# Row fetches that address x by bytes, with two rooms each, in a gather-bound graph layer

## The reference, cut to what matters

```
all_msgs = einsum('nh,thd->ntd', h, message_W) + message_b     # 8 edge types
msg      = all_msgs[src, edge_type]
messages = segment_sum(msg, dst, num_segments=12500)
gi = messages @ gru_w_ih.T + gru_b_ih ;  gh = h @ gru_w_hh.T + gru_b_hh
r = sigmoid(i_r + h_r); z = sigmoid(i_z + h_z); n = tanh(i_n + r * h_n)
out = layernorm(h + (1 - z) * n + z * h)
```

## Time and profile before

| | |
|---|---|
| median of three runs | 2633.79 us |
| span of the profiled execution, first to last instruction | 1973.7 us |
| the profiled execution's own time | not given by the page |
| median less span | 660.1 us |
| busy: POOL (GpSimd), PE (TensorE), DVE (VectorE), ACT (ScalarE) | 75%, 69%, 63%, 30% |
| share of the 16 DMA engines | about 25% |

### The profile page before, as it was taken

How to read it: one execution, slowest core, us unless ns; L and a number is a source line. 1 busy time by engine, 2 the same in 40 slices (tenths; PEclk the granted TensorE clock), 3 DMA queues, 4 the chain that set the end, 5 groups by cost and what they waited for, 6 DMA issues and landing times.

```text
span 1973.7 us, 39661 instructions
## 1 busy us (share of the span) xinstructions
PE 1356.7 (69%) x6561; PEld 1050.8 (53%) x6657; DVE 1248.0 (63%) x4650; ACT 594.6 (30%) x1489; POOL 1474.7 (75%) x1565
## 2 busy tenths in 40 slices
PE   1766676767676767676767676766667776767676
PEld 1755555555555555555555555555555554555554
DVE  7788366656565656565656565666566665656565
ACT  2423523232323232323232323232232323232322
POOL 7777777777777777777777777777777777777774
PEclk9878778888888888888888888888788888888888
DMA  5222222222222222222222222222222222222221
GB/s 128 59 63 64 60 61 65 64 66 64 66 65 64 66 62 67 62 67 62 67 63 66 62 67 63 65 65 65 65 65 65 65 65 65 65 65 64 65 63 42
DMA packets 103994, 128.78 MB, mean 65 GB/s; under 512 B 35152, under 2 KB 78495, under 8 KB 103806
## 3 DMA queue, kind: packets, MB, share of 16 engines
q0 software_dynamic: 49696, 101.88, 20.6%
q1 hardware_dynamic: 50328, 23.94, 4.4%
q10 hardware_dynamic: 3782, 0.93, 0.2%
HBM read 120.16 MB, written 6.40 MB: 64 GB/s over the span
## 4 chain that ended last, share of the span: by engine, by line
POOL 65%; issue 22%; DVE 8%; PE 3%; ACT 1%; DMA 1%; DVEq 0%; SPq 0%; ACTq 0%; POOLq 0%
POOL rows L697 32%; POOL rows_other L697 32%; DVE work L1354 1%; DVE codes L1351 1%; PE agg L1691 1%; DVE onehot L1187 1%; PE msg L1718 1%; DMA work<-in_src_dram 0%; PE msg L1836 0%; DVE root_a L1261 0%; DVE messages_T L1203 0%; ACT sums_room L763 0%; PE turn L1773 0%; ACT agg L763 0%; DVEq L1194 0%
## 5 line engine op out<-in xcount | busy, mean ns | idle before, releaser
L697 POOL DMA_INDIRECT rows<-in_x_dram,src_T x843 | 800.2, 949 | 258.8 <-issue 256.5
L697 POOL DMA_INDIRECT rows_other<-in_x_dram,src_T x675 | 638.1, 945 | 205.9 <-issue 205.9
L1691 PE MATMUL agg<-onehot,rows 128*128 128x128 f32 x1714 | 288.3, 331 | 250.1 <-DMA rows<-in_x_dram,src_T 248.5
L1718 PE MATMUL msg<-sums_room,w_type 128*128 128x320 f32 (+1 forms) x1552 | 439.9, 439 | 11.4 <-issue 7.1
L1691 PEld LDWEIGHTS agg<-onehot,rows 128*128 128x128 f32 x1714 | 259.8, 236 | 270.2 <-issue 269.1
L1691 PE MATMUL agg<-onehot,rows_other 128*128 128x128 f32 x1350 | 224.6, 326 | 230.5 <-DMA rows_other<-in_x_dram,src_T 229.0
L1718 PEld LDWEIGHTS msg<-sums_room,w_type 128*128 128x128 f32 x1552 | 302.6, 203 | 121.3 <-issue 27.2
L1236 DVE SCALAR_TENSOR_TENSOR sums_room<-turn,x_turned 128x128 f32<-128x128 f32 x696 | 145.8, 282 | 309.5 <-PE turn L1737 309.5
L1691 PEld LDWEIGHTS agg<-onehot,rows_other 128*128 128x128 f32 x1350 | 200.9, 231 | 248.2 <-issue 248.1
L763 ACT ACTIVATE sums_room<-agg 128x512 f32<-128x512 f32 x293 | 173.2, 591 | 364.4 <-PE agg L1691 264.3
L1187 DVE TENSOR_TENSOR onehot<-code_T,codes 128x640 f32<-128x640 f32 (+1 forms) x294 | 245.2, 863 | 18.2 <-PE agg L1691 18.2
(11 more groups left out here) (221 smaller groups left out, 1333.3 us busy)
## 6 DMA issues: line engine op xcount, KB each, us to landing
rows<-in_x_dram ACTq DMA_DIRECT2D x1792, 0.5 KB
w_hh_rows<-in_x_dram SPq DMA_DIRECT2D x1664, 0.5 KB
rows<-in_x_dram,src_T POOLq DMA_INDIRECT x843, 2.6
rows_other<-in_x_dram,src_T POOLq DMA_INDIRECT x675
x_next<-in_x_dram SPq DMA_DIRECT2D x97, 64.0 KB
out_dram<-out_tile SPq DMA_DIRECT2D x97, 64.0 KB
x_tile<-in_x_dram SPq DMA_DIRECT2D x96, 64.0 KB
work<-in_dst_dram SPq DMA_DIRECT2D x1, 609.4 KB
```

What stands on the lines that cost most here:

```text
L697: nc.gpsimd.indirect_dma_start(out=to, out_offset=None, in_=x[:, :], in_offset=bass.IndirectOffsetOnAxis(ap=index, axis=0),).then_inc(done ...
L1691: last = nc.tensor.matmul(agg[c][:, ds(offs[c][k] * TYPES, CODES)], tile_rows, onehot[c][:, k, :], start=False, stop=True, skip_group_chec ...
L1718: nc.tensor.matmul(msg[:, 0:cols], w_type[:, t, :], sums[:, t, 0:cols], start=t == 0, stop=False, skip_group_check=True)
```

## The change

1. The copies that make the tables of row numbers multiply them by 512 (`scale=float(ROW_BYTES)`), and there are two tables, `fetch_src` for ScalarE and `sync_src` for SyncE, since the two engines now fetch tiles of different places. SyncE waits for both (`fetch_src_ready, 2`).
2. A fetch takes 512 bytes of x, seen as a row of bytes, from the register's value on, and writes 512 bytes to the room.
3. Each engine has two rooms, used in turn.
4. SyncE's tile is place 7 (in group 1) instead of 15. ScalarE's stays at place 15. The rounds stay the same: 17, 23, ..., 95 and 20, 26, ..., 92. In a group TensorE takes the fetched tile last.
5. The rows are shared out over the blocks in another way: of the twelve blocks from the second one of a target round to the first one of the next, ScalarE weighs 5 (first) and 3 (second), SyncE 1 and 2, rounded to fours. That gives ScalarE 12 or 16 rows in a first block and 8 in a second (12 twice), SyncE 8 in a first and 12 or 16 in a second (8 ahead of round 20). Work on a first tile starts in the second block of round 12.
6. The waits that guard a room are for the tile before last: `tiles_done[2]` at the target of m-2, plus one.

```
+    ROW_BYTES = 4 * P
+    FETCH_STEPS, SYNC_STEPS = (6,), (6,)
+    FETCH_FIRST, SYNC_FIRST = EARLY + 6, EARLY + 9
+    FETCH_SHARE, SYNC_SHARE = (5, 3), (1, 2)
+    FETCH_PLACES, SYNC_PLACES = (15, 11, 7), (7, 15, 11)
...
+    def share_rows(rounds, share):
+        shares, before = {}, EARLY + 1
+        for m, target in enumerate(rounds):
+            places = [(r, half) for r in range(before, target + 1) for half in (0, 1)][1:-1]
+            weight, done, a = sum(share[half] for _, half in places), 0, 0
+            for place in places:
+                done += share[place[1]]
+                b = P * done // weight // 4 * 4
+                shares[place] = (m, a, b)
+                a = b
...
+        x_bytes = x.rearrange("n d -> (n d)").bitcast(U8)
-        sync_room = w_hh_rows[:, 0, :]
+        sync_rooms = [w_hh_rows[:, 0, :], w_hh_rows[:, 1, :]]
+        fetch_rooms = [rows[:, SPARE_SLOT, :], w_hh_rows[:, 2, :]]
...
-                        copy(fetch_src[0:ROWS, :], src_words[:, FETCH_SLOT * P:(FETCH_SLOT + 1) * P]).then_inc(fetch_src_ready, 1)
+                        for to, slot in ((fetch_src, FETCH_SLOT), (sync_src, SYNC_SLOT)):
+                            nc.scalar.activation(to[0:ROWS, :], src_words[:, slot * P:(slot + 1) * P], ACT.Copy,
+                                                 scale=float(ROW_BYTES)).then_inc(fetch_src_ready, 1)
...
             def fetch_rows(r, behind):
-                m, step = divmod(r - EARLY - 1, FETCH_EVERY)
...
+                m, begin, end = FETCH_SHARES[r, behind]
+                if begin == 0:
                     act.wait_ge(fetch_index_in[m % 2], (m // 2 + 1) * 16)
-                    act.dma_start(rows[p:p + 1, SPARE_SLOT, :], x[ds(number, 1), :]).then_inc(fetched[m % 2], 16)
+                    if m > 1:
+                        act.wait_ge(tiles_done[2], FETCH_ROUNDS[m - 2] + 1)
+                for a in range(begin, end, LOADED):
...
+                        act.dma_start(fetch_rooms[m % 2][p:p + 1, :].bitcast(U8),
+                                      x_bytes[ds(first, ROW_BYTES)].rearrange("(o n) -> o n", o=1)).then_inc(fetched[m % 2], 16)
...
             def gather_packed(r):
-                    for k in range(start, start + n - (c == 2 and (fetches(r) or sync_fetches(r)))):
+                    for k in range(start, start + n):
+                        if k - start in fetched_tiles(r, c):
+                            continue
...
             def sum_tiles(r, c, offs):
+                apart = fetched_tiles(r, c)
+                for k in [k for k in range(n) if k not in apart] + apart:
```

More of the change, by code:

```diff
@@ L9 @@
 I32 = mybir.dt.int32
+U8 = mybir.dt.uint8
 ALU = mybir.AluOpType
@@ L430, in fetches, with fetched_tiles @@
             return isinstance(r, int) and r in FETCH_ROUNDS
+        def fetched_tiles(r, c):
+            places = (fetch_place(r),) * fetches(r) + (sync_place(r),) * sync_fetches(r)
+            return [place - START[c] for place in places if START[c] <= place < START[c] + GROUPS[c]]
         def other(r):
@@ L581, in sync_rows @@
                     if m > 0:
-                        sp.wait_ge(tiles_done[2], r)
-                        if m + 1 < len(SYNC_ROUNDS):
+                        sp.wait_ge(tiles_done[2], SYNC_ROUNDS[m - 1])
+                        if m > 1:
+                            sp.wait_ge(tiles_done[2], SYNC_ROUNDS[m - 2] + 1)
+                        if m + 1 < len(SYNC_ROUNDS) and m > 0:
                             load_sync_index(m + 1)
-                _, numbers = nc.values_load_multi_w_load_instructions(
-                    sync_index[0:1, m % 2, a:a + n], engines=[sp.engine], min_val=0, max_val=NODES - 1,
-                    skip_runtime_bounds_check_because="row numbers, as the gathers take them")
@@ L588, in sync_rows @@
-                for p, number in enumerate(numbers, a):
-                    sp.dma_start(sync_room[p:p + 1, :], x[ds(number, 1), :]).then_inc(sync_fetched[m % 2], 16)
+                for a in range(begin, end, LOADED):
+                    _, numbers = nc.values_load_multi_w_load_instructions(
+                        sync_index[0:1, m % 2, a:min(a + LOADED, end)], engines=[sp.engine], min_val=0,
+                        max_val=(NODES - 1) * ROW_BYTES,
+                        skip_runtime_bounds_check_because="first bytes of rows, whose numbers the gathers take")
+                    for p, first in enumerate(numbers, a):
+                        sp.dma_start(sync_rooms[m % 2][p:p + 1, :].bitcast(U8),
+                                     x_bytes[ds(first, ROW_BYTES)].rearrange("(o n) -> o n", o=1)).then_inc(sync_fetched[m % 2], 16)
@@ L622, in _ @@
                     round_(r)
-                sp.wait_ge(fetch_src_ready, 1)
+                sp.wait_ge(fetch_src_ready, 2)
                 sp.wait_ge(bias_in, PARTS * 16)
@@ L1666, in landed @@
                 alike = range(EARLY + other(r), r + 1, 2)
-                left_out = sum(fetches(q) or sync_fetches(q) for q in alike) if c == 2 else 0
+                left_out = sum(len(fetched_tiles(q, c)) for q in alike)
                 return (0 if other(r) else (EARLY - 2) * EARLY_GROUPS[c]) + len(alike) * GROUPS[c] - left_out
```

81 lines of the change are left out of this document (48 added, 33 removed).

## The result

| | before | after |
|---|---|---|
| median, us | 2632.6 | 2452.85 |
| runs, lowest to highest | 4, 2624.72 to 2634.89 | 4, 2441.25 to 2468.42 |
| ratio after / before, 95% interval | | 0.9327 [0.9273, 0.9381] |

The change makes the kernel 6.7% faster, 180 us. I had forecast 2634.0 us and no change, with a range of 2622 to 2641 us.

The account below looks back on a forecast made before the run. GpSimd's gathers, 1.252 us each, were taken as the bound, hiding the fetches' saving. Span 1973.7 + 0 + 0.2 (one more copy at the start) = 1973.9 us, plus 660.1 us carried over, gave 2634.0 us; range 2622 to 2641 us.

Parts of the forecast that it names:

- the sum: Whole kernel: span 1973.7 + 0 + 0.2 = 1973.9 us, plus 660.1 us outside the span carried over, gives 2634.0 us.
- the cover: Fetch rounds: ScalarE's and SyncE's fetch issuing lies hidden behind GpSimd's gathers, so its saving is worth 0 us.
- cases of 0.06 each: Three rivals at 0.06 each: dearer byte fetches (2926 us), fetch issuing that counts (2516 us), 660 us growing with instructions (2577 us).
- GpSimd waits for nobody: From 241.84 to 1929.11 us GpSimd bounds: 1348 gathers by 1.252 us, with only one wait, of 1.9 us.
- The byte addresses: ScalarE's and SyncE's fetches: the multiplication goes, 70 ns saved per fetch, 0.378 to 0.308 us; worth 0 us, being hidden.
- The price of an instruction: At each fetch: FUSED_REGOPS of 37 ns plus its gap of 33 ns, 70 ns in all.
- Number of gathers, place, packets: 1553 tiles gathered before and after; SyncE's place 7 costs 0; two packets per fetch on q10 if the byte view is unsplit.
- Rooms and shares: Fetch blocks: two rooms with older guards, and other row shares with one more register load, all hidden, 0 us.
- C: Rival, faster: ScalarE's and SyncE's issuing counts in the timed execution; 118 us go, 2516 us; chance 0.06.
- D: Rival, faster: the 660 us grow with instructions; 3456 fewer is 8.7%, 57 us, giving 2577 us; chance 0.06.
- B: Rival, slower: the byte view makes each DMA_DIRECT2D longer, ScalarE's first block enters the loop; far end 2926 us; chance 0.06.
- A: The forecast itself: no change, 2634 us, as GpSimd's gathers bound the kernel; chance of same 0.77.

Follow-up runs that it names:

- six versions: Changed kernel (0.9327), it without fetches (0.9191), with ScalarE's alone (0.9213), with place 15 (0.9328), without fetches plus SyncE no-operations (0.9316); kernel before with byte addresses alone (0.9337).
- the probes: Separate programs doing none of the reference's work: no-operations alone, or beside GpSimd's gathers, loads, single-row transfers or small computing; starts counted, no ratio to the kernel before.
- the straight probe: Separate program of no-operations alone, written out, 1200 per engine in each of five stretches; 3340 starts in 40 us, none held.
- the probe of loops: The same no-operations in five stretches, each engine's 1200 as a loop of 12 times 100; none held, longest 18 ns from 160 to 200 us.

## Why the prediction was wrong, point by point

**The step that failed** is in the sum: "no row says what that is. I carry it over unchanged", of the 660.1 us between the span and the median. There is no such part. The profile of the same kernel among its timed runs has a span 1.7 us short of its time, and rounds of 26.1 us where I had read 19.5. With that the cover fell, too, behind which the sum put the fetches' saving at 0 us: the gathers of GpSimd, which I took for the bound, wait for the others in the timed runs. A missing quarter of the time was a reason to doubt the whole reading; I gave it to cases of 0.06 each.

**What bounds the kernel.** "GpSimd waits for nobody" is true of the first profile alone. As timed, GpSimd waits 383 us for others between 600 and 2000 us, and SyncE's chain of fetch instructions binds: taking ScalarE's 5376 fetch instructions away changes nothing (1.0016), while one more no-operation for each of SyncE's fetches costs 154 us, even on top of the first.

**The byte addresses.** The multiplication and nothing else goes, as I said: no FUSED_REGOPS at L636, MOVE and DMA_DIRECT2D at 29 and 228 ns as before. The worth, "0 us", was wrong. It is 6.6% (0.9337), measured alone.

**The price of an instruction.** I had 70 ns for the FUSED_REGOPS with its gap. In the timed runs one more start ahead of each of SyncE's fetches costs 93 to 107 ns of the kernel's time, whether it is 37 or 13 ns long. That starts are held for 0.70 or 1.40 us beside back-to-back gathers is shown; how that comes to about 100 ns for each is not.

**Number of gathers, place, packets.** Right: 1565 operations of GpSimd before and after, 0.9328 with place 15, 3782 packets on q10 in both, so the byte view came out unsplit, as the word view did.

**Rooms and shares.** 0 us forecast; without the byte addresses 17 us measured (0.9934), a small miss; with them no difference that sessions can tell (0.9337 and 0.9327).

**The rivals.** C, "ScalarE's and SyncE's issuing counts in the timed execution", was the right one, at 0.06. Its 118 us came from durations of the undisturbed profile; 180 were measured. And it's SyncE that counts first, where C took ScalarE's blocks. The gain ends at a level that six versions share: 0.919 to 0.934 with all fetches, ScalarE's, or none. What binds there is open. D, "the 660 us grow with the instructions", fails: ScalarE's 5376 taken away bring nothing, 4080 on an idle SyncE cost 1.2% at most. B fails by the durations (DMA_DIRECT2D's median 228 ns on SyncE and 213 on ScalarE in both kernels). A's own condition for being wrong, "the 660 us around the span, so large that the timed execution might have another bound than the profiled one", is what happened.

## What to carry to other kernels

Set the span of a profile against the timed median before reading anything else; a gap of a quarter means that the profile shows another execution than the one that is timed, and its slack, its chain and its prices are not those of the runs. Where SyncE or ScalarE issues beside back-to-back gathers of GpSimd, count the engine's instructions, not their durations alone: take register work out of the loop of an engine whose transfers somebody waits for, and ask whether hand-issued transfers still pay at all (without any this kernel took 2417.5 us, against 2433.8 with them).

## What the runs showed of the hardware

- In the probes, while GpSimd's gathers follow each other every 1.17 to 1.25 us, a start on SyncE, ScalarE or VectorE comes only every 1.38 to 1.40 us, no-operations of 13 ns too, once 15 to 25 us of gathers have gone by. At a pace of 1.46 us SyncE has a start in 0.134 us, at 1.94 us one in 0.056 us. 32 rows do as much as 128 (1.17 us a gather); ScalarE's loads of as many rows do nothing. In the kernel before as timed, 873 of SyncE's 4992 starts at its fetches took over 0.6 us.
- 83 starts a us on four engines, without gathers, hold nothing.
- What stays open: why the first profile of the kernel before, with gathers 1.252 us apart for 1687 us, shows no held start (no register instruction of a fetch over 51 ns), while every later profile of that kernel and of the changed one does; and whether the recording of instructions and transfers has a part in it.
- A wait in front of a no-operation did not hold it back in the straight probe (the no-operations of all four engines began within 1 us of the start); in the probe of loops the stretches kept their order.
